# One bank for each feed-forward pass, triangular masks of 64, and a new written order in a fused two-attention kernel

## The chip, the cores and the metric

The kernel runs on one core of a Trainium2 chip. The metric is the device time of one execution in microseconds (us). A difference of about 1% is what a measurement of this kernel can tell from no change.

## What is computed

Eight sequences of 256 tokens with 128 features go through four residual layers, each behind a layer norm: a causal attention over all 256 tokens with rotary positions (16 heads of 8), a feed-forward network (FFN) whose operands are rounded to FP4 in blocks of 16, a causal attention inside windows of 32 tokens, and the same FFN again.

```python
x = L0_attn_a_x                                    # (8, 256, 128)
x = x + _L0_attn_a_ref(_layernorm(x), Wq, Wk, Wv, Wo)
x = x + _L0_ffn_ref(_layernorm(x), w_gate, w_up, w_down)
x = x + _L0_attn_b_ref(_layernorm(x), w_qkv, ln_w, w_proj)
x = x + _L0_ffn_ref(_layernorm(x), w_gate, w_up, w_down)
# _L0_ffn_ref: h = silu(q4(x) @ q4(w_gate).T) * (q4(x) @ q4(w_up).T); out = q4(h) @ q4(w_down).T
# _L0_attn_a_ref: softmax(q k^T / sqrt(8) + causal mask) v, 16 heads
```

## The kernel before

One sequence is a batch b, from 0 to 7. It passes through stages: `front1` to `front3` (the first attention), `ffn_a1` to `ffn_a3` (first FFN, "a"), `local1` and `local2` (the windowed attention), `ffn_b1` to `ffn_b3` (second FFN, "b"). The batches overlap: while batch b is in the front, earlier ones are further on.

**Order.** Each engine runs its instructions in one fixed order. `weave` builds it: each stage of each batch is a Python generator that yields between steps, and the table `TIMES` gives each step a number. `TIMES["pe.ffn_a2"]`, line 4 for instance, holds the places of the steps of stage ffn_a2 of batch 3 among all of TensorE's steps. Semaphores (`wait_ge`) keep the engines in step; an instruction that waits holds everything behind it on its engine.

**Front.** In `front2` each head's scores (three 128x128 blocks, since the block above the diagonal is left out) are made twice: once with queries on the partitions, from which VectorE takes the row maxima (`bmax`, L1360), and in `front3` with keys on the partitions, from which ScalarE takes the exponential (`prob`, L1083). Each time TensorE runs four matmuls into one bank of PSUM: two for the scores (256 and 128 columns) and two that add the causal mask as a product of half an identity (`eye_lo`, `eye_hi`) with a mask of -1e30 (256 and 128 columns: L840, L841 and L871, L872). `front2` takes banks 0 and 1 of `fb` by turns, `front3` banks 2 and 3. The stacks `Qf`, `Kf` have 48 rows of a head (`NSTACK`) and three rows for the negated maximum.

**FFN.** `ffn1` normalizes and quantizes x (`xq`, made on GpSimd from `xw`). `ffn2` transposes `xq`, and for each of the two token tiles t runs a gate matmul (L975), a tanh (L1159), VectorE's `(th+1)*gate` (L1482, semaphore `s_hg`), an up matmul (L979) and the product `h` (L1486, `s_h_ready`). `ffn3` quantizes h (VectorE L1290 to L1503, ScalarE's Abs and Exp, GpSimd L1259 and L1266), transposes it (L991), multiplies with `wdT` (L997) and adds to x (L1507, `s_done`). In the last two batches (`SPLIT`) ffn3 goes tile by tile.

Both FFNs share the two banks of `ffb`: the gate goes to bank 0 and the up to bank 1. They take turns in the order of the list `FFN_TURNS`; a turn is an "up" (ffn2) or a "down" (the matmuls of ffn3) of one batch, and starts when the turn before is finished (`turn_before`). The last turns are `("b", 7, "up"), ("b", 6, "down"), ("b", 7, "down")`.

## Time and profile before

| | us |
|---|---|
| median of 3 runs | 422.82 (422.71 to 425.64) |
| the profiled execution, device time | 420.45 |
| its span, first to last instruction | 418.6 |
| TensorE busy | 327.8 (78%) |
| VectorE busy | 293.8 (70%) |
| ScalarE busy | 242.2 (58%) |
| GpSimd busy | 150.2 (36%) |
| mean granted clock of TensorE | 0.914 |

The span is a little shorter than the device time, which holds the start and the end of the launch too. Busy times of TensorE overlap: matmuls are pipelined, and a matmul's recorded time goes on past the start of the next one. PE is TensorE, DVE VectorE, ACT ScalarE, POOL GpSimd, SP the queue that issues DMAs.

### The profile page before, as it was taken

Reading aid. Unit: us, or ns where it says so; the run is one execution under the profiler, and the core shown is the slowest. Engines: PE = TensorE matmul, PEld = TensorE weight load, DVE = VectorE, ACT = ScalarE, POOL = GpSimd, SP = SyncE. Lnnn points to the kernel's source line nnn. Section 1 sums busy time; section 2 is a strip of 40 time slices with the busy share of each in tenths; the row PEclk is TensorE's granted clock in tenths of the full one; section 3 lists DMA queues with packets and bytes.
Section 4 is the critical chain, followed back from the end, with each engine's and each line's share of the span. In section 5 each row is a group of like instructions: output and inputs, shape, how many; then the busy total and the mean of one; then the engine's idle time right before and its main releaser. Section 6 shows DMA issues by size and latency. Waiting matters only on the chain.

```text
span 418.6 us, 9181 instructions
## 1 busy us (share of the span) xinstructions
PE 327.8 (78%) x3533; PEld 220.8 (53%) x3533; DVE 293.8 (70%) x746; ACT 242.2 (58%) x630; POOL 150.2 (36%) x210
## 2 busy tenths in 40 slices
PE   1416689778989997999999989997898676665844
PEld 1314446445666754767676666665457445453523
DVE  2835323839677889699987989788747867847741
ACT  2300064226578485488689789787669475592421
POOL 6230042213362037181572251603822553523323
PEclk9999968869899989999999999999699799998565
DMA  6252026605125025020451000000000000000000
GB/s 176 80 113 37 4 76 118 134 3 128 26 81 89 5 63 89 4 78 2 79 128 27 2 4 2 3 16 14 2 2 14 2 0 14 2 14 1 13 14 13
DMA packets 33103, 17.49 MB, mean 42 GB/s; under 512 B 1874, under 2 KB 32914, under 8 KB 33060
## 3 DMA queue, kind: packets, MB, share of 16 engines
q1 hardware_dynamic: 32772, 16.78, 18.3%
q8 instruction: 28, 0.46, 0.5%
q10 hardware_dynamic: 288, 0.13, 0.1%
q14 instruction: 15, 0.12, 0.1%
HBM read 9.37 MB, written 7.34 MB: 40 GB/s over the span
## 4 chain that ended last, share of the span: by engine, by line
PE 39%; DVE 25%; ACT 15%; issue 12%; POOL 4%; DMA 3%; SPq 2%; DVEq 0%; POOLq 0%; ACTq 0%
DVE bmax L1360 6%; PE fb L881 5%; PE fb L799 4%; PE ffb L997 4%; PE fb L869 3%; PE fb L838 3%; ACT prob L1083 2%; PE ffb L975 2%; PE lb L938 2%; PE ffb L991 2%; PE fb L888 2%; PE fb L871 2%; ACT Kd L1126 1%; PE fb L840 1%; PE ffb L979 1%
## 5 line engine op out<-in xcount | busy, mean ns | idle before, releaser
L1360 DVE TENSOR_REDUCE bmax<-fb 128x3 f32<-128x384 f32 x128 | 66.8, 549 | 20.7 <-PE fb L841 19.7
L1083 ACT ACTIVATE prob<-fb 128x384 f32<-128x384 f32 x128 | 59.3, 496 | 24.0 <-PE fb L872 23.3
L838 PE MATMUL fb<-Kf,Qf 48*128 48x256 bf16 x128 | 32.2, 300 | 13.3 <-DMA Kf<-scr_f 7.3
L869 PE MATMUL fb<-Qf,Kf 51*128 51x256 bf16 x128 | 31.3, 295 | 5.2 <-ACT prob L1083 4.4
L840 PE MATMUL fb<-maskb 64*128 64x256 bf16 x128 | 32.3, 300 | 0.0
L1222 POOL TENSOR_TENSOR qk<-ra,rb 128x512 f32<-128x512 f32 x7 | 8.9, 1272 | 63.9 <-DVE rb L1341 63.9
L871 PE MATMUL fb<-maskb 64*128 64x256 bf16 x128 | 31.1, 292 | 0.0
L881 PE MATMUL fb<-prob,Vf 128*32 128x128 f32 (+1 forms) x512 | 29.9, 354 | 1.4 <-ACT prob L1083 1.2
L838 PEld LDWEIGHTS fb<-Kf,Qf 48*128 48x128 bf16 x128 | 10.6, 94 | 31.3 <-DVE bmax L1360 17.5
L839 PE MATMUL fb<-Kf,Qf 48*128 48x128 bf16 x128 | 25.5, 234 | 0.0
L841 PE MATMUL fb<-maskb 64*128 64x128 bf16 x128 | 25.3, 232 | 0.0
L870 PE MATMUL fb<-Qf,Kf 51*128 51x128 bf16 x128 | 24.6, 230 | 0.0
L872 PE MATMUL fb<-maskb 64*128 64x128 bf16 x128 | 24.3, 227 | 0.0
L1259 POOL TENSOR_TENSOR fb__w<-fb__w,fb__c 128x704 f32<-128x704 f32 (+1 forms) x10 | 13.7, 1374 | 27.6 <-DVE fb__w L1503 27.6
L1259 POOL TENSOR_TENSOR fa__w<-fa__w,fa__c 128x704 f32<-128x704 f32 (+1 forms) x10 | 13.8, 1378 | 27.0 <-DVE fa__w L1503 27.0
L799 PE MATMUL fb<-xnTf,wT 128*128 128x256 f32 x64 | 21.5, 495 | 1.5 <-ACT xnTf L1011 1.5
L869 PEld LDWEIGHTS fb<-Qf,Kf 51*128 51x128 bf16 x128 | 10.6, 94 | 21.5 <-issue 8.8
L881 PEld LDWEIGHTS fb<-prob,Vf 128*32 128x32 f32 x512 | 14.4, 115 | 13.6 <-issue 4.5
L975 PE MATMUL ffb<-wguT,fb__xqT 128*128 128x352 f32 x32 | 17.0, 618 | 5.7 <-DVE fb__h L1482 4.0
L997 PE MATMUL ffb<-wdT,fb__hqT 128*128 128x128 f32 (+1 forms) x96 | 17.5, 336 | 4.9 <-ACT fb__hqT L1011 4.9
L1011 ACT ACTIVATE oTf<-fb 128x256 f32<-128x256 f32 x32 | 12.4, 387 | 14.3 <-PE fb L881 14.2
L1011 ACT ACTIVATE nmTf<-fb 48x256 bf16<-48x256 bf16 x8 | 3.0, 370 | 29.0 <-PE fb L846 29.0
(201 smaller groups left out, 962.7 us busy)
## 6 DMA issues: line engine op xcount, KB each, us to landing
scr_f<-partsf SPq DMA_DIRECT2D x16, 192.0 KB, 2.3
Qf<-scr_f SPq DMA_DIRECT2D x16, 192.0 KB, 3.6
Kf<-scr_f SPq DMA_DIRECT2D x16, 192.0 KB, 5.0
scr_f<-partsf SPq DMA_DIRECT2D x16, 128.0 KB, 1.9
xall<-in_L_attn_a_x_dram SPq DMA_DIRECT2D x8, 128.0 KB, 4.9
scr_f<-partsf SPq DMA_DIRECT2D x16, 64.0 KB, 1.6
out_dram<-xall SPq DMA_DIRECT2D x8, 128.0 KB, 1.8
ropet<-in_rope_dram SPq DMA_DIRECT2D x1, 512.0 KB, 4.1
```

Source lines behind the costliest of these rows:

```text
L799: mm = pe.matmul(fb[:, n // 2, (n % 2) * SEQ:(n % 2 + 1) * SEQ], wT[:, n, :], xnTf[:, :], start=True, stop=True)
L838: pe.matmul(S[:, 128:384], Qf[k, g, 128:256], Kf[k, g, 0:256], start=True, stop=True, skip_group_check=True)
L839: pe.matmul(S[:, 0:128], Qf[k, g, 0:128], Kf[k, g, 0:128], start=False, stop=True, skip_group_check=True)
L840: pe.matmul(ends(S, 0, 128), eye_lo[half_, :], twice(m_qk[half_, :]), start=False, stop=True, skip_group_check=True)
L869: pe.matmul(S[:, 128:384], Kf[k, g, 0:128], Qf[k, g, 0:256], start=True, stop=True, skip_group_check=True)
L871: pe.matmul(two(S[:, 0:256], 0, 128), eye_hi[half_, :], twice(m_kq[half_, :]), start=False, stop=True, skip_group_check=True)
L881: mm = pe.matmul(S[32 * j:32 * j + 32, k * P:SEQ], Vfs[b % RING][:, k, h, :], p, start=(k == 0), stop=(k == 1), skip_group_check=True)
L975: pe.matmul(ffb[:, 0, 0:I], w.xqT[:, t * P:(t + 1) * P], wguT[:, 0, :], start=True, stop=True).then_inc(w.s_g_ps, 1)
L997: mm = pe.matmul(ffb[:, t, 0:D], w.hqT[0:k, t, c, :], wdT[0:k, c, :], start=(c == 0), stop=(c == 2))
L1083: act.activation(prob[:, slot % 8, :], S[:, 0:384], ACT.Exp).then_inc(f.s_exp, 1)
L1259: pool.tensor_tensor(w.w[:, cols], w.w[:, cols], w.c[:, cols], ALU.subtract).then_inc(w.s_hdif, t1 - t0)
L1360: dve.tensor_reduce(bmax[:, h, 1:4], fb[:, h % 2, 0:384].rearrange("p (n k) -> p n k", k=P), AX.X, ALU.max).then_inc(bmax_done, 1)
```

## The change

1. **Masks.** The 128-wide mask matmul becomes 64 wide, so the two mask matmuls of a head have 2x64 columns each. What the wide one masked in full (a block of 64x64) goes into the score product itself: `Qf` and `Kf` get two more rows, in which q is 1 for tokens of the first or third block of 64 and k is -1e30 for those of the second or fourth. They are loaded once, by six more DMAs.
2. **Banks.** `FFN_TURNS` and `turn_before` go. In batches 0 to 5 (`LATE = 6`) FFN a works in bank 0 of `ffb` alone and FFN b in bank 1 alone, gate and up one after the other in the same bank. In batches 6 and 7 each has two banks of `fb`: a those of front2, once the last front2 is over, b those of front3, once the last front3 is over.
3. **Order.** Every table in `TIMES` is new.

```diff
-KROWS = NSTACK + 3
+MROWS = NSTACK + 2
+KROWS = MROWS + 3
+LATE = 6
...
+        def banks(w, b):
+            if b < LATE:
+                return [ffb[:, "ab".index(w.name), :]] * 2
+            first = 0 if w is ffn_a else 2
+            return [fb[:, first, :], fb[:, first + 1, :]]
+        def banks_free(w, b):
+            if b == LATE:
+                return (f_nmT, NBATCH) if w is ffn_a else (f.s_done, NBATCH)
+            return (w.s_done, T * b) if b > 0 else (fw_ready, 1)
...
-                    k = slice(64 * r, 64 * r + NSTACK)
+                    k = slice(64 * r, 64 * r + MROWS)
...
-                    pe.matmul(ends(S, 0, 128), eye_lo[half_, :], twice(m_qk[half_, :]), start=False, stop=True, skip_group_check=True)
-                    mm = pe.matmul(ends(S, 64, 64), eye_hi[half_, :], twice(m_qk[half_, 0:64]), start=False, stop=True, skip_group_check=True)
+                    pe.matmul(ends(S, 0, 64), eye_lo[half_, :], twice(m_qk[half_, :]), start=False, stop=True, skip_group_check=True)
+                    mm = pe.matmul(ends(S, 64, 64), eye_hi[half_, :], twice(m_qk[half_, :]), start=False, stop=True, skip_group_check=True)
...
             def ffn2(w, b):
                 yield
                 pe.wait_ge(w.s_xq_ready, b + 1)
-                if (turn_of := turn_before(w, b, "up")) is not None:
-                    pe.wait_ge(*turn_of)
+                pe.wait_ge(*banks_free(w, b))
+                A, B = banks(w, b)
+                turn(A, w.xq).then_inc(w.s_xqT_ps, 1)
                 for t in range(T):
                     yield
                     if t == 0:
                         pe.wait_ge(w.s_xqT_ready, b + 1)
+                    elif b < LATE:
+                        pe.wait_ge(w.s_h_ready, T * b + t)
                     else:
                         pe.wait_ge(w.s_hg, T * b + t)
-                    pe.matmul(ffb[:, 0, 0:I], w.xqT[:, t * P:(t + 1) * P], wguT[:, 0, :], start=True, stop=True).then_inc(w.s_g_ps, 1)
+                    pe.matmul(A[:, 0:I], w.xqT[:, t * P:(t + 1) * P], wguT[:, 0, :], start=True, stop=True).then_inc(w.s_g_ps, 1)
                     yield
-                    if t:
+                    if b < LATE:
+                        pe.wait_ge(w.s_hg, T * b + t + 1)
+                    elif t:
                         pe.wait_ge(w.s_h_ready, T * b + t)
...
             def ffn3(w, b):
...
-                        if t == 0:
-                            pe.wait_ge(*turn_before(w, b, "down"))
+                        if t and b < LATE:
+                            pe.wait_ge(w.s_hqT_ready, T * b + t)
...
     "dve.weights": """
-3 4 5 6 9 10""",
+4 6 8 9 14 15""",
```

Three places of the new order. A line number of the kernel after the change is 7 or 8 higher than that of the same instruction before.

**VectorE at the start**, from the first rotary product (`ra`) to the third part of batch 0's queries and keys (`partsf`); `fs`, `fu`, `fg` belong to the quantization of the FFN weights. Before:

```order
L1290 TENSOR_REDUCE fs<-fw 128x70
L1293 TENSOR_SCALAR fs<-fs 128x70
L1296 RECIPROCAL fs<-fs 128x70
L1304 TENSOR_TENSOR fu<-fw,fs 128x1120
L1340 TENSOR_TENSOR ra<-fb,ropet 128x512
L1341 TENSOR_TENSOR rb<-fb,ropet 128x512
L1346 TENSOR_TENSOR qk<-ra,rb 128x512
L1307 TENSOR_TENSOR fg<-fu,fa 128x1120
L1310 SCALAR_TENSOR_TENSOR lnw<-lnw 128x128
L1349 TENSOR_TENSOR restf<-qk,partsf 128x512
L1352 TENSOR_TENSOR partsf<-restf,partsf 128x512
```

With the change:

```order
L1348 TENSOR_TENSOR ra<-fb,ropet 128x512
L1349 TENSOR_TENSOR rb<-fb,ropet 128x512
L1298 TENSOR_REDUCE fs<-fw 128x70
L1354 TENSOR_TENSOR qk<-ra,rb 128x512
L1301 TENSOR_SCALAR fs<-fs 128x70
L1357 TENSOR_TENSOR restf<-qk,partsf 128x512
L1304 RECIPROCAL fs<-fs 128x70
L1312 TENSOR_TENSOR fu<-fw,fs 128x1120
L1360 TENSOR_TENSOR partsf<-restf,partsf 128x512
```

Batch 0 now goes ahead of most of the weights' work, and `fg` stands behind it. On TensorE the transposes of the weights (L774, L776 before), which stood ahead of the first head, now stand behind the second.

**TensorE in the middle**, FFN a of batch 3: with the change, from its gate matmul of tile 0 to its up matmul of tile 0.

```order
L980 MATMUL ffb<-wguT,fa__xqT 128x352
L919 MATMUL lb<-wqkvb,xnTl 128x256 x2
L925 MATMUL lb<-wqkvb,xnTl 32x32 x32
L853 MATMUL fb<-maskb,npartf 128x128 x2
L888 MATMUL fb<-prob,Vf 32x256 x4
L888 MATMUL fb<-prob,Vf 32x128 x4
L876 MATMUL fb<-Qf,Kf 128x256
L877 MATMUL fb<-Qf,Kf 128x128
L878 MATMUL fb<-maskb 128x2x64
L879 MATMUL fb<-maskb 128x2x64
L986 MATMUL ffb<-wguT,fa__xqT 128x352
```

Before, the up matmul stood right behind the gate matmul here; now other work of the local attention and the front stands between the two.

**VectorE at the end**, the quantization of h of batch 7 (`fb__scale` from `fb__h`) and the last additions of batch 6 (`xall`, twice 128x128). Before:

```order
L1482 SCALAR_TENSOR_TENSOR fb__h<-fb__th,ffb 128x352
L1486 SCALAR_TENSOR_TENSOR fb__h<-fb__h,ffb 128x352
L1507 TENSOR_TENSOR xall<-ffb,xall 128x128 x2
L1290 TENSOR_REDUCE fb__scale<-fb__h 128x22
L1293 TENSOR_SCALAR fb__scale<-fb__scale 128x22
```

With the change:

```order
L1515 TENSOR_TENSOR xall<-fb,xall 128x128 x2
L1490 SCALAR_TENSOR_TENSOR fb__h<-fb__th,fb 128x352
L1494 SCALAR_TENSOR_TENSOR fb__h<-fb__h,fb 128x352
L1298 TENSOR_REDUCE fb__scale<-fb__h 128x22
L1301 TENSOR_SCALAR fb__scale<-fb__scale 128x22
L1490 SCALAR_TENSOR_TENSOR fb__h<-fb__th,fb 128x352
```

The additions of batch 6, which stood behind all of batch 7's h, now stand ahead of it, and on TensorE and GpSimd the down pass of batch 6 stands ahead of the up pass of batch 7 in the same way.

## Rows read from the trace of the kernel before

**Rows 1.** Busy time by stretch; columns as in the first line.
```profile
core 0: us, PE busy (x) PEld busy (x) DVE busy (x) ACT busy (x) POOL busy (x), PEclk, DMA share, GB/s
...
77.70:175.80 98.10, 86.29 (x939) 56.97 (x936) 75.90 (x200) 56.64 (x143) 32.12 (x43) 0.91 0.30 62
175.80:288.60 112.80, 105.80 (x1440) 75.17 (x1440) 100.39 (x263) 90.95 (x249) 45.57 (x62) 1.00 0.15 33
288.60:325.00 36.40, 29.98 (x295) 19.50 (x295) 24.52 (x63) 28.11 (x74) 16.81 (x22) 0.91 0.02 5
325.00:358.10 33.10, 23.05 (x289) 15.78 (x291) 24.85 (x67) 20.42 (x55) 13.95 (x20) 0.90 0.02 5
358.10:386.00 27.90, 17.90 (x233) 11.78 (x218) 19.08 (x45) 15.68 (x44) 11.19 (x14) 0.96 0.02 6
386.00:418.60 32.60, 18.79 (x64) 13.10 (x64) 14.27 (x40) 9.80 (x21) 9.38 (x13) 0.55 0.04 13
```

**Rows 2.** Groups of instructions: count, busy us, mean ns, idle before.
```profile
L1360 DVE TENSOR_REDUCE bmax<-fb 128x3 f32<-128x384 f32 x128 | 66.8, 549 | 20.7 <-PE fb L841 19.7
L1159 ACT ACTIVATE fa__th<-ffb 128x352 f32<-128x352 f32 x16 | 7.6, 478 | 9.1 <-PE ffb L975 9.1
L1482 DVE SCALAR_TENSOR_TENSOR fa__h<-fa__th,ffb 128x352 f32<-128x352 f32 x16 | 8.2, 512 | 13.3 <-ACT fa__th L1159 13.0
```

**Rows 3.** TensorE in order of time: start, duration, instruction.
```profile
35.42 0.42 PE L840 MATMUL fb<-maskb 64*128 64x256 bf16 x1
35.63 0.31 PE L841 MATMUL fb<-maskb 64*128 64x128 bf16 x1
...
186.72 0.21 PE L870 MATMUL fb<-Qf,Kf 51*128 51x128 bf16 x1
186.78 0.27 PE L871 MATMUL fb<-maskb 64*128 64x256 bf16 x1
186.89 0.21 PE L872 MATMUL fb<-maskb 64*128 64x128 bf16 x1
```

**Rows 4.** The start, in order of time, on VectorE, GpSimd and TensorE.
```profile
14.74 0.68 DVE L1340 TENSOR_TENSOR ra<-fb,ropet 128x512 f32<-128x512 f32 x1
18.73 3.05 DVE L1349 TENSOR_TENSOR restf<-qk,partsf 128x512 f32<-128x512 f32 x1
22.48 1.80 DVE L1352 TENSOR_TENSOR partsf<-restf,partsf 128x512 bf16<-128x512 f32 x1 [0.70 <-ACT partsf L1011]
...
18.69 2.54 POOL L1203 TENSOR_TENSOR fg<-fg,fa 128x1120 f32<-128x1120 f32 x1 [10.36 <-DVE fg L1307]
...
10.27 3.78 PE L799 MATMUL fb<-xnTf,wT 128*128 128x256 f32 x8 [0.54 <-ACT xnTf L1011]
23.79 1.43 PE L774 MATMUL ffb<-identhm,fw 128*128 128x128 f32 x6 [7.09 <-POOL fw L1206]
25.02 0.84 PE L776 MATMUL lb<-identhm,fw 128*128 128x128 f32 x3
33.19 0.41 PE L838 MATMUL fb<-Kf,Qf 48*128 48x256 bf16 x2 [7.33 <-DMA Kf<-scr_f]
```

**Rows 5.** The chain that ended last: start, length, what.
```profile
5.26 0.27 SPq L705
...
53.55 0.71 ACT wguT L1011 x2
```

**Rows 6.** The end, in order of time, on GpSimd and VectorE.
```profile
391.28 0.62 POOL L1251 TENSOR_TENSOR fb__xq<-fb__xw,fb__xscale 128x256 f32<-128x256 f32 x1
...
398.40 0.52 DVE L1486 SCALAR_TENSOR_TENSOR fb__h<-fb__h,ffb 128x352 f32<-128x352 f32 x1
...
404.15 0.29 DVE L1507 TENSOR_TENSOR xall<-ffb,xall 128x128 f32<-128x128 f32 x1 [2.58 <-PE ffb L997]
404.36 0.51 DVE L1290 TENSOR_REDUCE fb__scale<-fb__h 128x22 f32<-128x352 f32 x1
...
408.00 0.93 POOL L1259 TENSOR_TENSOR fb__w<-fb__w,fb__c 128x352 f32<-128x352 f32 x1 [8.07 <-DVE fb__w L1503]
```

More of the change, by code:

```diff
@@ L64 @@
 0 1
-8 9
-11 12
-15 16
-19 20
-22 23
-25 27
-28 29""",
+7 8
+9 10
+14 15
+18 20
+23 24
+26 27
+28 30""",
     "sp.front2": """
-7
-14
-17
-21
-24
-26
-30
-31""",
+6
+11
+17
+21
+22
+25
+32
+33""",
     "sp.load": """
@@ L85 @@
 5
-6
-10
-13
-18""",
+12
+13
+16
+19""",
     "sp.store": """
-32
-33
+29
+31
 34
@@ new lines @@
+452 453 456 457 459 460 461 462 464 466 467 470 472 476 477 479 480 482 483 487 491 495 498""",
+    "pe.local1": """
+131 140 157
+204 209 220
+280 284 295
+335 338 355
+393 397 413
+454 458 469
+502 504 509
+528 530 533""",
+    "pe.local2": """
+164 167 173 174 179 187
+227 228 235 236 240 244
+300 301 311 316 322 328
+362 364 372 380 384 387
+424 430 440 446 449 451
+475 478 486 489 497 500
+512 513 521 522 525 526
+538 540 544 545 546 547""",
+    "pe.ffn_a2": """
+71 74 83 88 92
+123 127 144 152 162
@@ new lines @@
+198 203 210 214 222
+279 283 288 291 293
+327 330 340 344 350
+388 392 398 403 409
+463 465 468 473 474
+505 506 507 508 510""",
+    "pe.ffn_b2": """
+213 223 230 239 254
+314 318 325 329 336
+373 376 379 385 391
+434 437 447 450 455
+488 494 499 501 503
+520 524 527 529 531
+532 534 535 536 537
+552 553 554 555 556""",
+    "pe.ffn_a3": """
+114 116 118 119
+177 180 185 186
+238 241 245 249
+315 320 323 324
+370 374 377 378
+436 439 442 443
+490 492 493 496
+515 518 519 523""",
+    "pe.ffn_b3": """
@@ L243 @@
-217 220 226
-279 283 287
-327 331 333
-363 364 367""",
-    "act.ffn_b1": """
-129 133
-208 223
-243 247
-278 298
-308 315
-357 361
-384 386
-399 402""",
-    "act.ffn_b2": """
-148 160 170
-234 241 245
-258 263 269
-305 312 318
-354 356 359
-378 379 382
+168 177
+213 219
+261 263
+312 320
+357 362""",
+    "act.ffn_a2": """
+42 45 56
+76 81 98
+129 134 142
+184 189 197
+226 230 239
+267 271 279
+326 330 334
+365 367 370""",
+    "act.ffn_b1": """
+128 136
+166 194
+233 236
+270 286
+316 337
+360 364
@@ L263 @@
+384 388
+403 405""",
+    "act.ffn_b2": """
+144 147 159
+214 222 227
+258 260 266
+300 304 311
+351 354 358
+380 382 386
 391 393 395
[L264 removed]
+407 408 409""",
     "act.ffn_a3": """
[L266 to L281 removed]
+65 68 71
+106 113 117
+151 158 161
+202 216 220
+251 256 259
+293 303 306
+338 346 352 353
@@ L282 @@
+372 373 377 379""",
+    "act.ffn_b3": """
+188 203 205
+238 250 253
+276 288 291
+323 341 345
+366 374 375
+392 396 398
+401 402 404 406
 410 411 412 413""",
     "pool.weights": """
-1 2""",
+2 3""",
     "pool.front1": """
 0
-3 4 5 6
+1 4 5 6
 7 8 9 10
 11 14 15 16
-17 22 23 26
-27 28 29 33
-34 39 41 44
-45 51 52 53""",
+17 23 24 25
+26 30 31 33
+34 42 43 46
+47 54 57 58""",
     "pool.local1": """
-20 24
-38 43
-48 58
-60 65
-67 72
-83 84
-90 94
-101 105""",
+22 27
+36 39
+45 51
+61 63
+70 72
@@ L303 @@
+79 81
+91 95
+103 105""",
     "pool.ffn_a1": """
 12 13
-21 25
-30 31
-40 47
-56 59
-68 69
-77 82
-89 92""",
-    "pool.ffn_b1": """
-32 37
-57 61
-64 66
-73 74
-75 79
-93 95
+20 21
+32 35
+44 49
+59 60
+69 71
+80 82
+92 94""",
+    "pool.ffn_b1": """
+37 38
+48 53
+62 66
+75 76
+85 87
+93 96
 104 106
-109 110""",
+113 114""",
     "pool.ffn_a3": """
 18 19
-35 36
-42 46
-54 55
-62 63
-76 78
-85 86 87 88
-97 98 99 100""",
-    "pool.ffn_b3": """
-49 50
-70 71
-80 81
-91 96
-102 103
+28 29
+40 41
@@ new lines @@
+48 51 57
+103 105 112
+165 168 173
+240 242 249
+303 305 309
+376 377 386
+458 460 467
+516 518 523""",
+    "dve.local1": """
+123 124 127 144
+185 187 196 211
+255 261 275 297
+330 332 335 359
+394 396 403 429
+462 464 468 491
+522 524 529 553
+577 578 581 594""",
+    "dve.local2": """
[7 rows of a table added]
+603 604 605 606 607 608 611 613 619""",
+    "dve.ffn_a1": """
[7 rows of a table added]
+525 527 531 532 534 536 540 541""",
+    "dve.ffn_a2": """
+78 83 86 89
+135 139 147 155
+205 208 214 220
+293 294 296 299
+340 351 356 360
+413 421 426 430
```

335 lines of the change are left out of this document (125 added, 210 removed), and 104 rows, old and new, of tables (FFN_TURNS, TIMES).

## The prediction

> **What bounds the kernel now.** I read the stretches first [rows 1]. I cut the span at the ends of front3 of batches 0, 3, 6 and 7 (77.7, 175.8, 288.6, 325.0), at the start of local1 of batch 7 (358.1) and at the end of its local2 (386.0). From 175.8 to 288.6 TensorE is busy 105.8 of 112.8 us and VectorE 100.4: both are nearly full, TensorE a little more. From 77.7 to 175.8 TensorE has 86.3 of 98.1, at a granted clock of 0.91, and VectorE only 75.9; TensorE is the bound there. After 325.0 nothing is full (VectorE 24.9 of 33.1, then 19.1 of 27.9, then 14.3 of 32.6): one chain runs through FFN a, the local attention and FFN b of batch 7, and what lengthens it is work of earlier batches that stands ahead of it in the order of an engine. So a removed matmul is worth its full time up to 288.6 at most, and nothing after 325.0; there only the order counts.
>
> **The masks.** In TensorE's own sequence the start of the next matmul after a 256-column one comes 0.11 us later (186.78 to 186.89) and after a 128-column one 0.06 later (186.72 to 186.78) [rows 3]. Early, while matmuls still run at half speed, the 256-column mask takes 0.21 (35.42 to 35.63) [rows 3]. A head's pass thus loses 0.05 us, at half speed 0.1. There are 128 heads (16 by 8 batches) [rows 2] with two passes each: 256 passes, 13.7 us of TensorE's time at full clock. Three 128-column matmuls with weights of their own now follow each other; the row at 186.72 has such a matmul spaced by 0.06 with a weight load behind it, so I expect no floor above that. Five more rows of contraction change no column count and are taken at nothing. The maxima on VectorE (0.549 us a head, 66.8 in all [rows 2]) stay.
>
> **The start, to 77.7.** Four edits. First, VectorE. Batch 0's rotary product can begin when the projection on TensorE is over (10.27 + 3.78 = 14.05), and began at 14.74 [rows 4]. With the change: ra and rb 14.1 to 15.4, the reduction of the weights (1.3 us, about the time of the other 1120-column operations) to 16.8, qk to 17.5, a copy on ScalarE of 0.6, and then restf. This one took 3.05 us, while an operation of the same 128x512 size took 0.68; GpSimd was in an operation of 2.54 that began at 18.69, in the same moment [rows 4]. In the new order GpSimd's work on the weights comes later, since fg stands behind, so I give restf and the third part 0.7 each. With the rest of the weights' steps between, partsf ends at 21.6 and not at 24.3: 2.7 us earlier for the writes, the loads and the first head, which the chain leads through. The Trainium skill has the rule behind the slow restf (SBUF — State Buffer, section "SBUF: two separate sides"): a VectorE operation with two SBUF inputs and a GpSimd operation that reads SBUF exclude each other for a whole instruction. By that rule restf costs what the row for ra shows; without it the gain here would be some 1 us less.
>
> Second, the transposes of the weights, 23.79 to 25.86 [rows 4], ran for nothing while TensorE waited for the first head's operands (33.19); now they stand behind the second head and wait for GpSimd's later result. They take 2.1 us, of which 0.7 lies in the wait for the maximum: a loss of 1.4. Third, ScalarE's copy of the weights stood in the chain at 53.55 with 0.71 [rows 5]; it now comes ahead of the front3 of batch 0, during the projection of batch 1: a gain of 0.7. Fourth, six more DMAs are issued on the SP queue, at 0.27 plus a hop of 0.04 each [rows 5]: the weights land 1.9 later, at about 13.2, before VectorE wants them at 15.4, so nothing. Masks: in front2 of batch 0 two banks alternate and each pair of heads gives back 0.1, 0.8 in all; in front3 of batch 0 another 0.7. Sum: -2.7 + 1.4 - 0.7 - 0.8 - 0.7 = **-3.5** (bounds -5 and 0).
>
> **The middle, 77.7 to 325.0.** Here I counted, in both orders, the steps between the same marks, with the mean duration of each (for TensorE at full clock, start to start). In the first stretch the new order brings work forward: one more local2, the up pass of FFN b of batch 0 for the greater part, and 2.4 us of FFN a's down matmuls. TensorE's sum goes from 82.6 to 89.2 although the masks take 4.8 off, VectorE's from 80.3 to 91.9. TensorE is the bound of that stretch, so it gets longer by 6 (bounds: 0 if its idle 12 us take it up, +12 if VectorE becomes the bound). In the second the work is gone again: TensorE 112 to 103, VectorE 113 to 105. These sums stand for 105.8 and 100.4 of busy time [rows 1], since neighbouring instructions overlap; both fall by 8 to 9. I take -8 (bounds -10 and -4). In the third, 36.4 us, TensorE 29.8 to 28.6, VectorE 23.1 to 24.6: -1 (bounds -2 and +1.5). Sum of the middle: **-3**.
>
> **One bank for an FFN.** In batches 0 to 5 the up matmul now waits for tanh (0.478) and the first product (0.512) [rows 2], about 1.1 with hops; the second gate waits for the product after it, 0.6; the transposes of the second h tile wait for a copy, 0.6. Less what the second gate waited before, that is 3.1 us more for each of twelve FFNs. I cost it at nothing, for the order shows the cover: between gate and up of batch 3 stand two local projections, a transpose, an output group and a head of front3, some 3 us. Where the bank is not shared any more, a pass need not stand behind the other FFN's turn. If this cover is gone, it is the slower rival below.
>
> **The end, after 325.0.** From 325.0 to 358.1 the order before had 28.0 us of VectorE steps and 25.9 of TensorE ahead of local1 of batch 7; now 23.3 and 21.2, since the down pass of b of batch 3 and part of the up of batch 4 come before the mark. The chain of one FFN without queueing is some 22 us (the last one takes 30, of which 8 are a wait, below), so 33.1 has room: **-3.5** (bounds -4.7 and 0). From 358.1 to 386.0 VectorE has 18.4 and then 19.6: 0 (bounds -1 and +2). In the last stretch the h of batch 7 was ready at 398.92, but its first scale reduction started at 404.36, behind the addition of batch 6 at 404.15, and GpSimd got its input at 408.00 [rows 6]. Now batch 6 goes first. GpSimd's four steps for it (3.6 us) put xq of batch 7 at 394.5 and not 391.9, and TensorE must wait for the last addition of batch 6, about 396.1: the up pass is 4.2 us later and h is ready at 403.1. Its quantization then starts at once and reaches GpSimd at 406.0: **-2** (bounds -5, if batch 6 is done earlier, and +1).
>
> **Sum.** -3.5 - 3 - 3.5 - 2 = -12.0. Against the profiled execution, 420.45, this is 408.4; that execution lay 2.4 below the median of 422.8, which less 12.0 is 410.8. I say **410**. The bounds of the steps, added in quadrature about the sum, give 404 to 416 for this case.
>
> **Rivals.**
> *VectorE is the bound everywhere* (for it: 100.4 of 112.8 [rows 1], and nothing of its work is removed). Then the first stretch costs +12, the second gives -8, the third +1.5, with the start and the end as above: -3.5 + 5.5 - 5.5 = -3.5, some **419**. Against it: VectorE has 22 us idle in the first stretch.
> *The clock takes it back.* The granted clock is 1.00 where TensorE is fullest and 0.91, 0.90 and 0.55 where it is busy less [rows 1]. If lighter matmul work made the second stretch fall to 0.91, its 105.8 us would grow by about 10, with what else is gained some **418**. The Trainium skill (TensorE: Matmul & The Clock Gate, Part 1) states it as a rule: the slow clock is the default and activity releases it; less work can thus run slower. Against it: work is also packed closer.
> *The one bank stalls TensorE.* All twelve FFNs exposed in full are 12 x 3.1 = 37 us; half exposed, 18.5, makes **429**. TensorE is in order, so the waiting up matmul holds the front's heads, and VectorE with them. From one third exposed the gain of 12 is gone. Against it: the steps placed between.
> *More is gained.* The first stretch takes the moved work into idle time (0 for +6), the end gives its bounds: -3.5 - 9 - 4.7 - 5 = -22, some **400**.
> *The masks give nothing*, because the weight load sets the pace of a short matmul: excluded by the spacing of 0.06 at 186.72 [rows 3].
>
> **Chances.** Forecast 0.55, more gained 0.17, VectorE 0.11, clock 0.07, stalls 0.10. The range 398 to 421 leaves out the stalls and a part of the great gain. Within 1% is 418.6 to 427, about what a measurement can tell from no change; most of the VectorE and a part of the clock case falls there: faster 0.78, same 0.13, slower 0.09.
>
> **What would show it.** The mask matmuls spaced by 0.06, not 0.11; partsf at about 21.6 and restf near 0.7; front3 of batch 0 ending near 74, of batch 3 near 178, of batch 6 near 283, of batch 7 near 318; local1 of batch 7 starting near 348 and b's first h reduction right behind h. Wrong would be: idle time of TensorE before the up matmuls (L986) of more than some 5 us in all up to batch 5, a granted clock below 1.00 in the middle, or front3 of batch 3 ending after 184.

## The result and the profile after

The changed kernel takes **408.8 us** (406.1 to 410.2, four runs) against 422.8 for the kernel before on the same chip: ratio **0.969** [0.960, 0.979]. A second measurement of the same two kernels gave 0.971 [0.966, 0.975]. The forecast was 410. The ratios of all tables leave out single executions more than 1.5% above the fastest of their kernel; the medians are those of all.

The profiled execution took 409.7, its span is 407.8. First the stretches between the same marks as in [rows 1]: end of front3 of batches 0, 3, 6 and 7, start of local1 of batch 7, end of its local2. Busy time by stretch in the kernel after, columns as there:

```profile
73.10:180.60 107.50, 93.03 (x1124) 64.45 (x1122) 82.76 (x227) 67.52 (x178) 38.67 (x50) 0.91 0.28 58
180.60:290.00 109.40, 101.12 (x1284) 71.49 (x1283) 91.08 (x246) 82.55 (x220) 46.58 (x62) 0.96 0.15 34
290.00:324.90 34.90, 31.00 (x361) 20.86 (x361) 24.58 (x65) 27.25 (x74) 12.94 (x17) 0.85 0.03 10
324.90:352.20 27.30, 20.72 (x215) 14.43 (x214) 21.43 (x60) 18.63 (x50) 13.22 (x19) 0.81 0.02 6
352.20:377.80 25.60, 17.60 (x203) 11.44 (x201) 18.72 (x49) 16.05 (x44) 7.55 (x11) 0.93 0.02 6
377.80:407.80 30.00, 15.23 (x46) 10.10 (x46) 11.82 (x31) 7.93 (x17) 9.36 (x12) 0.59 0.03 9
```

| stretch | before | after | difference | forecast |
|---|---|---|---|---|
| to the end of front3(0) | 77.7 | 73.1 | -4.6 | -3.5 |
| to front3(3) | 98.1 | 107.5 | +9.4 | +6 |
| to front3(6) | 112.8 | 109.4 | -3.4 | -8 |
| to front3(7) | 36.4 | 34.9 | -1.5 | -1 |
| to local1(7) | 33.1 | 27.3 | -5.8 | -3.5 |
| to local2(7) | 27.9 | 25.6 | -2.3 | 0 |
| to the last addition (416.3, 405.6) | 30.3 | 27.8 | -2.5 | -2 |
| sum | | | -10.7 | -12 |

The front of batch 7 ends at 324.9, where it ended before (325.0). So the middle used up all that the start had won; the whole net gain was made behind it, where part of the work that used to stand there (the b passes of batches 3 and 4) had been done in the middle. The granted clock is the second thing to see: 0.96 and 0.85 where [rows 1] has 1.00 and 0.91. The record of the clock knows two levels, 1.00 (2.4 GHz) and 0.50 (1.2 GHz); what lies between is the mean of a stretch. (The mark of local1 of batch 7 is the end of the last addition of FFN a of that batch, 358.2 before and 352.2 after.)

VectorE at the start of the kernel after, in order of time, which answers to [rows 4]:

```profile
14.10 0.69 DVE L1348 TENSOR_TENSOR ra<-fb,ropet 128x512 f32<-128x512 f32 x1 [5.12 <-PE fb L806]
...
17.91 0.69 DVE L1357 TENSOR_TENSOR restf<-qk,partsf 128x512 f32<-128x512 f32 x1 [0.59 <-ACT partsf L1019]
...
20.38 0.68 DVE L1360 TENSOR_TENSOR partsf<-restf,partsf 128x512 bf16<-128x512 f32 x1
...
30.66 1.02 DVE L1368 TENSOR_REDUCE bmax<-fb 128x3 f32<-128x384 f32 x2 [5.79 <-PE fb L848]
33.32 1.02 DVE L1368 TENSOR_REDUCE bmax<-fb 128x3 f32<-128x384 f32 x2 [1.64 <-PE fb L848]
34.69 1.02 DVE L1368 TENSOR_REDUCE bmax<-fb 128x3 f32<-128x384 f32 x2 [0.34 <-PE fb L848]
```

restf is down from 3.05 to 0.69, and partsf ends at 21.06 and not at 24.28: 3.2 us. The wait between the first and the second pair of maxima, in which TensorE runs the weights' transposes, is 1.64, against 0.34 at every later pair: 1.3 us.

TensorE in order of time in the middle, which answers to [rows 3]:

```profile
185.87 0.22 PE L846 MATMUL fb<-Kf,Qf 50*128 50x128 bf16 x1
185.92 0.22 PE L847 MATMUL fb<-maskb 64*128 64x128 bf16 x1
185.98 0.21 PE L848 MATMUL fb<-maskb 64*128 64x128 bf16 x1
```

The narrow masks do start 0.05 to 0.06 after each other. The up matmul of the FFNs in one bank, with what TensorE sat idle for before it (us, times):

```profile
L986 PE MATMUL ffb<-wguT,fa__xqT x24: 459/459/563, 90.2 to 268.7; 128*128 128x352 f32 x24
...
  issue: 2.5, 11
  DVE fb__h L1490: 0.8, 3
  DVE fa__h L1490: 0.6, 2
  DVE fb__h L1494: 0.5, 2
```

So the waits for products before the up matmul came to 1.9 us in the whole kernel; before the change they were 6.6. The same for the gate matmul, waits for VectorE alone, first before, then after:

```profile
L975 PE MATMUL ffb<-wguT,fa__xqT x32: 458/460/564, 90.7 to 342.8; 128*128 128x352 f32 x32
...
  DVE fb__h L1482: 11.5, 10
  DVE fa__h L1482: 5.1, 7
```

```profile
L980 PE MATMUL ffb<-wguT,fa__xqT x24: 459/459/563, 86.5 to 266.0; 128*128 128x352 f32 x24
...
  DVE fa__h L1490: 4.4, 2
  DVE fb__h L1490: 3.2, 3
...
  DVE fb__h L1494: 1.4, 3
...
  DVE fa__h L1494: 1.1, 5
```

They fell from 16.6 to 10.1 us. And the end, on VectorE and GpSimd, which answers to [rows 6]:

```profile
387.39 0.29 DVE L1515 TENSOR_TENSOR xall<-fb,xall 128x128 f32<-128x128 f32 x1 [2.57 <-PE fb L1005]
391.04 0.52 DVE L1490 SCALAR_TENSOR_TENSOR fb__h<-fb__th,fb 128x352 f32<-128x352 f32 x1 [3.35 <-ACT fb__th L1167]
391.79 0.52 DVE L1494 SCALAR_TENSOR_TENSOR fb__h<-fb__h,fb 128x352 f32<-128x352 f32 x1 [0.23 <-PE fb L986]
392.34 0.52 DVE L1298 TENSOR_REDUCE fb__scale<-fb__h 128x22 f32<-128x352 f32 x1
...
397.25 0.93 POOL L1267 TENSOR_TENSOR fb__w<-fb__w,fb__c 128x352 f32<-128x352 f32 x1 [11.15 <-DVE fb__w L1511]
```

The addition of batch 6 comes first (387.39), the scale reduction stands right behind h (392.34 behind 391.79; before 5.4 us lay between), and GpSimd has its input 4.9 us after h, where it took 9.1 before.

### The profile page after: what moved, and what is told of

Read it like the earlier page. It is cut to its first block, busy times and chain, and to the rows that moved or that the text cites. A ratio compares the mean times of both kernels' runs of the same rounds, so it can differ in the third digit from the quotient of the medians.

```text
span 407.8 us, 9171 instructions
## 1 busy us (share of the span) xinstructions
PE 320.2 (79%) x3533; PEld 220.0 (54%) x3533; DVE 281.9 (69%) x746; ACT 240.9 (59%) x630; POOL 149.2 (37%) x210
## 3 DMA queue, kind: packets, MB, share of 16 engines
q1 hardware_dynamic: 32820, 16.85, 18.2%
## 4 chain that ended last, share of the span: by engine, by line
PE 36%; DVE 23%; ACT 14%; issue 11%; POOL 7%; DMA 5%; SPq 4%; DVEq 0%; POOLq 0%; ACTq 0%
DVE bmax L1368 5%; PE fb L806 4%; PE fb L888 4%; DMA Kf<-scr_f 4%; PE ffb L1005 3%; PE fb L845 3%; ACT prob L1091 2%; PE lb L945 2%; PE ffb L986 2%; PE fb L876 2%; PE ffb L980 2%; SPq L742 2%; SPq L733 1%; DMA scr_f<-partsf 1%; PE fb L1005 1%
## 5 line engine op out<-in xcount | busy, mean ns | idle before, releaser
L1368 DVE TENSOR_REDUCE bmax<-fb 128x3 f32<-128x384 f32 x128 | 65.9, 548 | 18.8 <-PE fb L848 18.2
L1091 ACT ACTIVATE prob<-fb 128x384 f32<-128x384 f32 x128 | 58.9, 495 | 27.0 <-PE fb L879 26.5
L845 PE MATMUL fb<-Kf,Qf 50*128 50x256 bf16 x128 | 32.5, 301 | 25.6 <-DMA Kf<-scr_f 17.9
L876 PE MATMUL fb<-Qf,Kf 53*128 53x256 bf16 x128 | 30.1, 287 | 3.9 <-ACT prob L1091 3.2
L845 PEld LDWEIGHTS fb<-Kf,Qf 50*128 50x128 bf16 x128 | 10.7, 94 | 40.7 <-DMA Kf<-scr_f 18.4
L847 PE MATMUL fb<-maskb 64*128 64x128 bf16 x128 | 25.7, 235 | 0.0
L846 PE MATMUL fb<-Kf,Qf 50*128 50x128 bf16 x128 | 25.5, 234 | 0.0
L848 PE MATMUL fb<-maskb 64*128 64x128 bf16 x128 | 25.3, 232 | 0.0
L878 PE MATMUL fb<-maskb 64*128 64x128 bf16 x128 | 23.7, 225 | 0.0
L877 PE MATMUL fb<-Qf,Kf 53*128 53x128 bf16 x128 | 23.5, 223 | 0.0
L879 PE MATMUL fb<-maskb 64*128 64x128 bf16 x128 | 23.3, 222 | 0.0
L876 PEld LDWEIGHTS fb<-Qf,Kf 53*128 53x128 bf16 x128 | 10.1, 93 | 21.8 <-issue 9.5
L945 PEld LDWEIGHTS lb<-Kd,Qd 128*128 128x128 f32 x128 | 19.7, 220 | 1.2 <-issue 0.4
L1019 ACT ACTIVATE nmTf<-fb 48x256 bf16<-48x256 bf16 x8 | 3.1, 387 | 27.9 <-PE fb L853 27.9
L945 PE MATMUL lb<-Kd,Qd 128*128 128x128 f32 x128 | 19.4, 301 | 0.0
L806 PEld LDWEIGHTS fb<-xnTf,wT 128*128 128x128 f32 x64 | 15.6, 255 | 6.3 <-ACT xnTf L1019 3.4
```

What stands on the lines that cost most here:

```text
L806: mm = pe.matmul(fb[:, n // 2, (n % 2) * SEQ:(n % 2 + 1) * SEQ], wT[:, n, :], xnTf[:, :], start=True, stop=True)
L845: pe.matmul(S[:, 128:384], Qf[k, g, 128:256], Kf[k, g, 0:256], start=True, stop=True, skip_group_check=True)
L846: pe.matmul(S[:, 0:128], Qf[k, g, 0:128], Kf[k, g, 0:128], start=False, stop=True, skip_group_check=True)
L847: pe.matmul(ends(S, 0, 64), eye_lo[half_, :], twice(m_qk[half_, :]), start=False, stop=True, skip_group_check=True)
L848: mm = pe.matmul(ends(S, 64, 64), eye_hi[half_, :], twice(m_qk[half_, :]), start=False, stop=True, skip_group_check=True)
L876: pe.matmul(S[:, 128:384], Kf[k, g, 0:128], Qf[k, g, 0:256], start=True, stop=True, skip_group_check=True)
```

## The experiments

Each was timed in five rounds beside the kernel before; "before" is the median of that kernel in the same runs, so kernels with the same number there shared a chip and were timed together. e7 and c3 ran on the chip of 420.4 too, at another time.

| kernel | median us | before | ratio | interval |
|---|---|---|---|---|
| after_again | 409.7 | 420.4 | 0.971 | [0.966, 0.975] |
| e1_masks_only | 423.9 | 421.5 | 1.006 | [1.002, 1.009] |
| e2_wide_masks_in_after | 410.8 | 421.5 | 0.972 | [0.967, 0.976] |
| e3_start_only | 419.0 | 421.5 | 0.993 | [0.990, 0.996] |
| e4_end_only | 415.5 | 421.5 | 0.987 | [0.984, 0.990] |
| e5_no_masks_in_after | 414.6 | 420.4 | 0.986 | [0.983, 0.990] |
| e7_columns_back | 406.4 | 422.3 | 0.959 | [0.954, 0.964] |
| e6_half_max_in_after | 403.3 | 420.4 | 0.959 | [0.956, 0.963] |
| v1_tail_and_weights | 403.6 | 420.4 | 0.960 | [0.956, 0.965] |
| c1_fill_start | 412.3 | 422.4 | 0.974 | [0.969, 0.979] |
| c2_fill_start_end | 412.7 | 422.4 | 0.956 | [0.951, 0.960] |
| c3_fill_end_only | 402.1 | 422.3 | 0.945 | [0.941, 0.949] |

The six executions of some kernels spread widely. The ratio of e7 stands on four of them (401.6 to 406.7; the others 411.2 and 414.2), that of c2 on two (402.2 and 404.3; the others 412.4 to 418.0), that of c3 on three (396.8 to 400.3; the others 403.9 to 406.2). For these I go by the medians of all six, divided by before's: e7 0.962, c1 0.976, c2 0.977, c3 0.952, beside v1 0.960, the changed kernel 0.975 and e5 0.986.

**The masks alone, in the kernel before.**

```diff
-pe.matmul(ends(S, 0, 128), eye_lo[half_, :], twice(m_qk[half_, :]), ...)
+pe.matmul(ends(S, 0, 64), eye_lo[half_, :], twice(m_qk[half_, :]), ...)
```

and the rows, loads and waits that belong to them, as in the diff ahead; banks and order stay.

> The narrow masks alone, in the order and with the banks of before. Theory M (TensorE is the bound up to 288.6, so its removed time is worth most of itself): 13.7 us come off TensorE, the time falls by 8 to 13, to about 412. Theory O (the gain of the change is in its order and banks; in the old order TensorE, VectorE and ScalarE wait for each other in turn, so a lighter TensorE only waits more): 1.5 us at the start, where matmuls run at half speed, and 1 to 3 behind it, to about 418 to 420.

Measured: 1.006, no gain and a slight loss, worse than both theories. Busy time by stretch between the ends of front3 of batches 0, 3, 6 and 7:

```profile
77.50:174.30 96.80, 85.34 (x939) 58.13 (x936) 74.47 (x200) 56.81 (x143) 32.09 (x43) 0.88 0.31 62
174.30:289.20 114.90, 105.76 (x1439) 75.81 (x1440) 100.44 (x263) 90.86 (x249) 45.53 (x62) 0.97 0.15 32
289.20:327.90 38.70, 30.95 (x295) 20.63 (x294) 24.83 (x64) 28.15 (x74) 16.96 (x22) 0.87 0.02 5
```

The first stretch is 1.3 us shorter than before, the two others 2.1 and 2.3 longer, and the granted clock is lower in all three (0.88, 0.97, 0.87 against 0.91, 1.00, 0.91). TensorE's busy time is the same as before (105.76 against 105.80) although the columns of 96 passes by 0.05, some 5 us, are gone from it. In the first 77.5 us the masks gave 0.2 where the prediction has 1.5. The 3% below 1.00 in the second stretch are some 7 us at half clock, which can lose 3.4 us of work at most. So even at full clock the narrow masks would have won at most 1.4 of the 5 us there.

**The changed kernel with the wide masks.** The same edit backwards.

> The kernel after with the wide masks of before, all else kept. Theory M: it loses the 13.7 us again, to about 419 to 421. Theory O: it loses 3 to 6, to about 412 to 415.

Measured: 0.972 against 0.971 of the changed kernel, less than either theory had. With the new order too, the 13.7 us of columns are worth nothing that can be measured; the intervals leave room for some 2 us each way.

**The new start alone.** In the kernel before, only the places in the order of the weights' steps and of batch 0's:

```diff
 dve.weights, then dve.front1 of batch 0
-3 4 5 6 9 10
+2.2 2.4 2.6 2.7 15.1 15.2
-0 1 2 7 8 11 12
+0 1 2 2.1 2.3 2.5 2.8
 act.weights, pool.weights, pe.weights
-1 8
+4.1 6.5
-1 2
+3.1 3.2
-3
+5.5
```

> Before, with only the start in the new order (batch 0 ahead of the weights on VectorE, GpSimd and ScalarE; the weights' transposes behind the second head). If the start shifts everything behind it: 2.0 us less (2.7 earlier operands, 1.4 lost to the transposes, 0.7 for ScalarE's copy), some 420 to 421, with the third part of batch 0 ready at about 21.0 and the operation restf at 0.7 us. If the gained time is lost in waits behind it: no change, 422 to 423, although front2 of batch 0 ends earlier.

Measured: 0.993, 2.5 us by the medians. Batch 0 shows what was expected of it (restf 0.69, partsf done at 21.06, front3(0) at 74.5). In this profiled execution, 415.2 us and so 3.8 below the kernel's median, the win of the start was still there at the end of front3(7) (319.7 against 325.0); where the other executions lose part of it isn't shown.

**The new end alone.** In the kernel before, VectorE's quantization of the last h goes ahead of the additions of batch 6:

```diff
 dve.ffn_b3 of batch 6:
-621 622 623 624 625 626 627 628 630 632 635 636
+621 622 623 624 625 626 627 628 630 632 644.5 646.5
+                    if w is ffn_b and b == NBATCH - 1:
+                        dve.wait_ge(w.s_hq_ready, T * (b - 1) + t1)
```

> Before, with only the last stretch changed: on VectorE the quantization of h of batch 7 stands ahead of the two additions of batch 6, and waits for the tile of batch 6 on GpSimd instead. Theory O: h of batch 7 reaches GpSimd at 402 and not 408, and the end comes 4 to 6 earlier, some 417 to 418.5. Rival: TensorE's or GpSimd's own queue holds the last down matmuls, so less than 1.5 us is gained, some 421 to 423.

Measured: 0.987, 6.0 us by the medians, the upper end of theory O. This edit moves VectorE's order alone; in the changed kernel the down pass of batch 6 goes ahead on TensorE and GpSimd too. VectorE in order of time:

```profile
399.53 0.52 DVE L1486 SCALAR_TENSOR_TENSOR fb__h<-fb__h,ffb 128x352 f32<-128x352 f32 x1
399.97 0.51 DVE L1290 TENSOR_REDUCE fb__scale<-fb__h 128x22 f32<-128x352 f32 x1
...
403.61 0.28 DVE L1509 TENSOR_TENSOR xall<-ffb,xall 128x128 f32<-128x128 f32 x1
```

The reduction now starts right behind h and not behind the addition. Start and end alone give 2.0% together; the changed kernel has 2.9%. The 0.9% that is left goes to banks and the rest of the order by subtraction, which takes for granted that the parts add up; it was not tried apart.

**No causal masks in the blocks of 64.** The changed kernel without its two mask matmuls in either pass; the scores inside those blocks are then unmasked.

```diff
-pe.matmul(ends(S, 0, 64), eye_lo[half_, :], twice(m_qk[half_, :]), ...)
-mm = pe.matmul(ends(S, 64, 64), eye_hi[half_, :], twice(m_qk[half_, :]), ...)
```

> The kernel after without the two mask matmuls of each head and pass (it leaves out the causal mask inside the blocks of 64): 256 more columns of TensorE go for each of 256 passes, 27 us at full clock, twice what the change took. If TensorE's own time is the bound up to the end of the last front, the time falls by 12 or more, below 397. Clock theory: less work lets the granted clock fall, matmuls of the middle run at half speed for a larger share, and the time falls by less than 5. Theory of the fixed order (every engine waits for the others in turn): falls by 3 to 7, with a granted clock as in the kernel after.

Measured: 414.6, 4.9 us *slower* than the changed kernel with 512 matmuls less, against all three theories. Nothing waits for a matmul that isn't there; what differs in the trace is the clock. Busy time by stretch between the same marks:

```profile
71.90:180.00 108.10, 89.99 (x922) 55.10 (x922) 82.12 (x227) 67.37 (x178) 38.61 (x50) 0.86 0.27 58
180.00:295.90 115.90, 103.10 (x1091) 64.63 (x1091) 92.05 (x246) 83.14 (x220) 46.51 (x62) 0.85 0.14 31
```

**The same columns without their meaning.** That kernel, with two matmuls of the same operands and 128 columns each put at the head of each pass, where the scores then overwrite them; the masks inside the blocks of 64 are still left out.

```diff
+pe.matmul(ends(S, 0, 64), eye_lo[half_, :], twice(m_qk[half_, :]), start=True, ...)
+pe.matmul(ends(S, 64, 64), eye_hi[half_, :], twice(m_qk[half_, :]), start=True, ...)
 pe.matmul(S[:, 128:384], Qf[k, g, 128:256], Kf[k, g, 0:256], start=True, ...)
```

> The changed kernel with its causal masks inside the blocks of 64 left out again, as in e5_no_masks_in_after, but with two matmuls of the same operands and the same 128 columns at the head of each pass, whose result the scores then overwrite: the same number of matmuls and of columns as the changed kernel, no mask. Theory (what made e5_no_masks_in_after slower is the missing columns, through the clock or through the pace of the passes, not the missing masks): time as the changed kernel within 1.5 us, ratio 0.967 to 0.974, half-clock time between 60 and 290 us of 30 to 45 us. Rival (the time goes by the masks themselves or by where they stand in a pass, or e5_no_masks_in_after was an accident of its placement): as e5_no_masks_in_after, 413 to 416, ratio 0.982 to 0.990.

Measured: 0.962 by the medians, where the kernel without these columns has 0.986 (10 us) and the changed kernel 0.975: the columns give back all that e5 had lost, and 5 us more than the theory said. The half-clock time between 60 and 290 us is 16 us, where 30 to 45 was expected. For the time it is of no matter whether the columns mask. Busy time by stretch, same marks:

```profile
75.20:180.80 105.60, 90.31 (x1129) 59.89 (x1128) 82.57 (x227) 67.42 (x178) 38.62 (x50) 0.95 0.28 59
180.80:285.90 105.10, 97.32 (x1279) 66.47 (x1280) 90.75 (x246) 82.56 (x220) 46.58 (x62) 1.00 0.16 35
285.90:318.00 32.10, 29.21 (x361) 19.44 (x360) 24.02 (x64) 26.72 (x74) 12.91 (x17) 0.89 0.04 11
```

The work of VectorE and ScalarE is the same in both kernels (90.75 and 82.56 against 92.05 and 83.14 in the second stretch); the one takes 105.1 us for it at a clock of 1.00, the other 115.9 at 0.85. The mean clock of the profiled executions was 0.875 against 0.820, that of all six 0.888 against 0.838. At the price of half clock that is estimated below, 0.2 us a us, the clock makes up some 7 of these 10.8 us; what makes the rest is not shown. That this kernel beats the changed one too, at equal columns, may come from its clock in this profile (1.00 against 0.96) or from the order inside the pass, which differs also; that was not taken apart.

**Less for VectorE.** The maxima over half the keys of each block; the bound of the softmax is then another.

```diff
-dve.tensor_reduce(bmax[:, h, 1:4], fb[:, h % 2, 0:384].rearrange("p (n k) -> p n k", k=P), ...
+dve.tensor_reduce(bmax[:, h, 1:4], fb[:, h % 2, 0:384].rearrange("p (n k) -> p n k", k=P)[:, :, 0:64], ...
```

> The kernel after with the row maxima taken over half of each block (it leaves out half of the keys from the maximum): VectorE's 128 reductions take about 0.35 us and not 0.55, 25 us less on VectorE, TensorE as it was. If VectorE is the bound of the front, the time falls by 8 to 15, to 394 to 401. If TensorE is, by less than 3, 406 to 408.

Measured: 6.4 us less than the changed kernel. The group of the maxima (busy us, mean ns, idle before) in this kernel:

```profile
L1368 DVE TENSOR_REDUCE bmax<-fb 128x3 f32<-128x192 f32 x128 | 41.0, 349 | 27.5 <-PE fb L848 26.9
```

and in the changed kernel:

```profile
L1368 DVE TENSOR_REDUCE bmax<-fb 128x3 f32<-128x384 f32 x128 | 65.9, 548 | 18.8 <-PE fb L848 18.2
```

VectorE is relieved of 24.9 us (65.9 to 41.0) and 8.7 of that becomes waiting for TensorE (18.2 to 26.9). By the medians a quarter of the relief reaches the end, so VectorE doesn't hold the bound alone. Where it arrives isn't shown: in the profiled execution, 406.8 and the slowest of the six, the time from front3(0) to front3(6) is 217.7 against 216.9 in the changed kernel, no gain at all.

**A better version.** The changed kernel with four edits: the weights' transposes behind the last head of batch 0 (place 5 to 19.5), FFN b of batch 7 in the banks of `ffb`, GpSimd's deviation of FFN b of batch 7 earlier, and the first h tile of batch 7 quantized ahead of its second product, with the last addition of batch 6 behind it (on TensorE the last down step of batch 6 goes from 551 to 556.5 for the same reason):

```diff
 dve.ffn_b3 of batches 6 and 7:
-610 612 614 615 616 617 618 620 623 624 631 632
-635 636 638 640 641 642 643 644 645 646 647 648
+610 612 614 615 616 617 618 620 623 624 631 645.5
+635 636 636.3 636.6 641 642 643 644 645 646 647 648
+            if w is ffn_b and b == NBATCH - 1:
+                return [ffb[:, 0, :], ffb[:, 1, :]]
```

> The kernel after, mended at two places: the transposes of the weights behind the last head of batch 0, where TensorE waits for VectorE (1.3 less); and FFN b of batch 7 in the two banks of the FFNs, which have been free since batch 5, so that its up pass needs not wait for the last addition of batch 6 (2.2 less), with GpSimd's step for its deviation first and the quantization of its first h tile closed before the second product (0.6 less). Sum 4.1: 403 to 406 where after has 408. If the start is lost in slack behind it, only the end's 2.8: 405 to 406.

Measured: 403.6, 6.1 us less than the changed kernel on the same chip by the medians, where 4.1 was the sum, and faster than both kernels. The profiled execution, 408.1 and so 4.5 above the median, shows the long wait at the second pair of maxima gone (0.34) and the last stretch at 26.5 for 27.8; where the rest comes from it doesn't show.

**Matmuls that only keep TensorE busy.** On that version:

```diff
+def filler(n, dst, cols=512):
+    for _ in range(n):
+        pe.matmul(dst[:, 0:cols], identb, maskb[:, 0:cols], start=True, stop=True, ...)
```

> The kernel of v1_tail_and_weights with matmuls added whose result nobody reads: 34 of 512 columns between the projection of batch 0 and its first head, and one of 256 columns after each head's second product in batch 0. They go to a PSUM bank that is free there. Theory (the clock follows what TensorE does, and that is what the narrow masks lost): the first 60 us ran 38.7 us at the half clock in the profile of v1_tail_and_weights; with TensorE busy there the record stays at full speed, the projections and scores of the first stretch take less time each, and the kernel ends 2 to 5 us earlier than v1_tail_and_weights did (about 399 to 401, ratio 0.950 to 0.955). Rival (the start is bound by VectorE's maxima, at 1.37 us a pair of heads, and the clock there prices nothing): the added columns only stand in front of the first head, some 7 to 14 us of TensorE work of which the wait for the statistics of batch 0 covers about 8; time as v1_tail_and_weights or up to 4 us more (404 to 407, ratio 0.960 to 0.968).

Measured: 0.976 against 0.960 by the medians, 6.8 us worse, and worse than the rival had it. The theory that busy matmuls keep the clock up failed here. TensorE in the filled stretches of c1, busy time by window:

```profile
15.00:25.00 10.00, 9.58 (x37) 4.36 (x38) 8.12 (x16) 4.01 (x5) 1.16 (x3) 1.00 0.35 98
30.00:50.00 20.00, 18.71 (x94) 10.41 (x95) 9.95 (x21) 1.20 (x4) 0.00 (x0) 0.50 0.01 1
```

The filler ran from 15.9 to 24.6. Its first six matmuls start 0.43 us apart, those from 18.42 on 0.22, so it did bring the upper level; the record of 1.00 ahead of that is no measurement. Then TensorE stood idle for 5.6 us behind the loads, and the record fell to 0.50 in that gap and stayed there for 24 us. TensorE was 94% busy from 30 to 50 by the profile, which counts a matmul's pipelined end as busy. The filler ahead of the loads cost next to nothing, since the first maximum came at 31.0 and not at 30.6. What cost was the 256 columns after each head: a head's maximum came every 0.97 us, where a pair took 1.37 in v1, 4.6 us over the 16 heads. These are as good as the whole loss in the profiled executions (412.4 against 408.1).

> The kernel of c1_fill_start with such matmuls in the last stretch too: 14 of 512 columns behind the last local projection, 2 behind each turn of the last FFN's input and of its hidden rows, 12 behind the last second product of batch 6. Theory (clock): the windows from 378 us on stood at a granted clock of 0.59 in the changed kernel, where TensorE is busy 12 of 30 us; with the filler the record stays near 1.00 and each matmul of the last two FFNs takes about half as long, some 5 of 12 us, of which 2 to 5 us lie on the chain at the end: about 395 to 398 us, ratio 0.940 to 0.948. Rival (the end is a chain of quantizations on VectorE and ScalarE, and the few matmuls between them are started too late for a faster clock to matter, or the filler stands in their way): as c1_fill_start within 1 us, or 1 to 3 us more.

Measured: median 412.7, no better than c1 and far from the theory's 395 to 398, but from the last local addition to the last addition of all 24.0 us against 26.5. So the start was taken out and the end kept:

> The kernel of v1_tail_and_weights with the filler of c2_fill_start_end in the last stretch alone, none at the start. In c2_fill_start_end the last local product of batch 7 to the last add took 24.1 us against 26.5 us in c1_fill_start and in v1_tail_and_weights, while the filler at the start moved every milestone back 4 to 8 us. Theory (at the end TensorE stands in the chain and half a clock costs it): 2.4 us less than v1_tail_and_weights, about 401 us, ratio 0.950 to 0.957, with the same 24.1 us between these two points and the granted clock of the last 35 us above 0.9. Rival (the 2.4 us in that profile came from where its clock happened to stand): time as v1_tail_and_weights, 403 to 405, ratio 0.958 to 0.963, and 26 us between the points.

Measured: 402.1, with 24.0 us between these two points and a clock of 0.90 over the last 35 us, as the theory had it. Busy time from the end of local2(7) to the last addition, first v1_tail_and_weights, whose row is followed by that of c3:

```profile
377.40:404.00 26.60, 14.85 (x46) 9.89 (x46) 11.85 (x31) 7.92 (x17) 9.75 (x12) 0.56 0.02 6
```

```profile
378.00:402.00 24.00, 18.16 (x78) 10.03 (x76) 11.86 (x31) 7.93 (x17) 9.76 (x12) 0.86 0.02 5
```

32 matmuls more, VectorE's and ScalarE's work the same, and the stretch is some 2.5 us shorter at a clock of 0.86 in place of 0.56. The last two additions show where, first v1, then c3:

```profile
400.75 0.29 DVE L1521 TENSOR_TENSOR xall<-ffb,xall 128x128 f32<-128x128 f32 x1 [3.86 <-PE ffb L1011]
403.62 0.29 DVE L1521 TENSOR_TENSOR xall<-ffb,xall 128x128 f32<-128x128 f32 x1 [2.58 <-PE ffb L1011]
```

```profile
399.87 0.29 DVE L1533 TENSOR_TENSOR xall<-ffb,xall 128x128 f32<-128x128 f32 x1 [2.80 <-PE ffb L1021]
401.72 0.29 DVE L1533 TENSOR_TENSOR xall<-ffb,xall 128x128 f32<-128x128 f32 x1 [1.55 <-PE ffb L1021]
```

VectorE waits 2.1 us less for the down matmuls. Here the clock was made faster on purpose and the time followed: this is shown, for this stretch, by two profiled executions with the filler (24.0 us in c2 and c3) and two without it (26.5 in v1 and c1). The whole kernel is at 0.952 against 0.960 by the medians, 3.3 us faster, with executions that overlap (396.8 to 406.2 against 402.1 to 408.5); it is the fastest that I have.

## Why the prediction was right

The total came out within 2 us, by luck in part: three of the seven terms lie beyond their bounds, in opposite directions.

**The bound.** Right in that TensorE doesn't hold the middle alone: a quarter of e6's relief of VectorE arrives. That a removed matmul is worth its full time up to 288.6 was called the most it can be worth, and then taken as its value (next paragraph). After 325.0 the order counts as forecast, 10.6 us came from there; but the pace of the matmuls counts as well, by c3 2.5 us in the last stretch, which the prediction had at nothing.

**The masks.** The count was right, the spacing of 0.05 to 0.06 too, the value was not. e1 (1.006) and e2 (0.972 against 0.971) show no gain. The step that failed is the sum of the second stretch, which took TensorE's sum "for TensorE at full clock" and let the time fall with it: forecast -8 (bounds -10 and -4), measured -3.4. VectorE's busy time fell as summed (100.4 to 91.1), TensorE's by 4.7 only (105.8 to 101.1). A clock below 1.00 in the middle was one of the prediction's own signs of being wrong. What it cost can be read from six profiled executions that have the same order and masks in this stretch:

| kernel | us | clock | TensorE busy |
|---|---|---|---|
| v1 | 108.4 | 0.97 | 99.5 |
| c3 | 108.5 | 0.97 | 99.9 |
| after | 109.4 | 0.96 | 101.1 |
| c1 | 110.8 | 0.91 | 103.9 |
| c2 | 111.5 | 0.91 | 104.7 |
| after_again | 112.1 | 0.90 | 104.8 |

A line through them gives, as an estimate, 0.2 us for each us at half clock, and at full clock some 107.3 us with 98 busy. TensorE's busy time would then have fallen by the 8 that were summed, and the time by 5.5. So of the 4.6 us that were missing the clock took some 2; the rest is busy time of TensorE that became waiting (idle 7.0 us before, some 9 by the line); for which engine was not taken apart. (e7 reached 105.1 us at 1.00, 7.7 less than before, but with another order inside the pass.) The clock's part is the rival "the clock takes it back", whose mechanism was given 0.07; it came, at about a fifth of the price (10 in the prediction), beside the forecast and not in its place. The Trainium skill (TensorE: Matmul & The Clock Gate, Part 1) has activity release the slow clock. e5 against e7 agrees: in the second stretch 0.85 without the columns and 1.00 with them. c1 does not: 94% busy for 20 us at 0.50. The measurement decides, so by these runs it isn't something that a stretch can count on.

**The first stretch.** +9.4 against +6, between the bounds (0, +12), though VectorE is busy for only 82.8 of the 107.5 us. The clock is the same as before (0.91), and TensorE's busy time grew as summed (86.3 to 93.0, forecast +6.6); but its idle time, taken as unchanged, grew from 11.8 to 14.5. In e7 the stretch has +7.5. The term was undersized by what the packed work waits; which wait it is was not taken apart.

**The start.** -4.6 against -3.5. restf at 0.69, partsf at 21.06 (forecast 21.6), the transposes at 1.3 (forecast 1.4) all came as worked out. By itself this order of the start ends front3(0) 3.2 us earlier, where 2.0 was summed, and is worth 2.5 us of the total by the medians (e3); the 1.5 for the masks came to 0.2 in e1. The trace agrees with the rule of the Trainium skill on VectorE and GpSimd (SBUF — State Buffer, "SBUF: two separate sides"): away from GpSimd's operation restf took what ra takes, 0.69 us.

**One bank.** Right at nothing: 1.9 us of waits for products before the up matmul in all, the gate's waits fell, and before the transposes of h (L998) TensorE waited 0.4 us for the copy. The slower rival is excluded by these rows.

**The end.** The three terms gave -5.8, -2.3 and -2.5 against -3.5, 0 and -2. The first lies beyond its bound of -4.7 and the second beyond its bound of -1. The backlog taken out of the first freed more than the sums of VectorE's and TensorE's steps (4.7 each). The second was costed at 0 by VectorE's sums alone (18.4 and 19.6), while GpSimd's busy time fell from 11.2 to 7.6 us; that this is the cause is not shown. These 5.1 us more than forecast are what made up for the middle. So the total, 10.7 against 12.0, came out right by errors of opposite sign: 7.5 us too much forecast in the middle, 5.1 too little at the end and 1.1 too little at the start.

**The range.** The bounds of the steps, added in quadrature about 408.4, give some 401 to 418 and not 404 to 416; the case was stated more narrowly than its own terms allow.

## What to carry to other kernels

Read a gain from where work is moved to, not only from what is removed: here 13.7 us of TensorE's columns went and brought nothing that could be measured, while moving a quantization ahead of two additions brought 1.3%. When TensorE work is cut in a kernel that lives near the full clock, look at the granted clock of the same stretches again before crediting the cut, and test it by putting the columns back without their meaning. Filler matmuls are worth trying in a stretch where TensorE is half idle and still stands in the chain; there they won 2.5 us. Ahead of a wait for loads they won nothing here, and between the heads that VectorE waits for they cost their own time.
